# Transposes of the down product ahead of the Hadamard transposes, its products between them and the Hadamard products, in one feed forward of a twelve-block decoder

## The chip, the cores and the metric

The kernel runs on one core of one Trainium2 chip. A core has five engines that each work off a queue of their own in order: TensorE (PE in the rows; PEld is its weight load), VectorE (DVE), ScalarE (ACT), GpSimd (POOL) and SyncE (SP), which here only starts DMAs. The metric is the device time of one launch in microseconds, the median of several runs. One further execution was taken with the hardware profiler; all rows come from it.

## The reference

A decoder of four layers with an attention, a cross attention and a feed forward each, `x = layernorm(x + block(x))` twelve times, on `x` of shape (4, 512, 512) in float32. The change touches one block, the feed forward of the second layer, which works on quantised activations and ternary weights and has a Walsh-Hadamard transform of length 2048 in front of its last product:

```python
def act_quant(x, bits=8):
    qb = 128.0
    scale = qb / jnp.clip(jnp.max(jnp.abs(x), axis=-1, keepdims=True), EPS)
    return jnp.clip(jnp.round(x * scale), -qb, qb - 1) / scale

def bitlinear(x, w):
    return jnp.einsum('bsh,oh->bso', act_quant(x), weight_quant(w))

def h_bitlinear(x, w):
    return jnp.einsum('bsh,oh->bso', act_quant(fwht(x)), weight_quant(w))

gate = bitlinear(x, w_gate)          # 512 -> 2048
up = bitlinear(x, w_up)              # 512 -> 2048
return h_bitlinear(jax.nn.silu(gate) * up, w_down)   # 2048 -> 512
```

## The kernel before

The 2048 rows of `x` stay on the chip as 16 tiles of 128 rows. Each block is a stage between two barriers: every engine waits at its start until all engines and DMAs are done with the stage before. The stage of this change is `l1_ffn`. No DMA is on its path; the weights are there.

Each tile `i` runs through a pipeline of rounds `t`. The table `LAG` says how many rounds after its start a tile is at a step, and `order(names)` walks, in each round, through the named steps in the order in which they are named. Each engine has a string of names of its own, so this string is the order of that engine's queue. The steps of one tile are:

- quant: VectorE quantises the tile of `x`, ScalarE writes it as bf16 (XB, L1775).
- turn: TensorE transposes it (4 transposes, L210 by way of `k.tr`), ScalarE copies it (XT, L1744).
- up: TensorE makes gate and up in four column blocks each, `g` and `u` in turn, 4 products of 128x512 a block (L205 by way of `k.mm`); ScalarE applies silu to `g` (L1751), VectorE multiplies with `u` into IM (L1805), which frees the bank of `u`.
- hadamard: TensorE transposes IM (the it transposes, 16 of 128x128 f32), ScalarE copies them (L1756); TensorE multiplies with the 128x128 Hadamard matrix (the ha products, 16, shown as 32 rows), ScalarE copies these (L1760). The four remaining levels over the 16 blocks are butterflies (L1694): two on VectorE, four instructions, and two on GpSimd, four instructions.
- stats, scale, clip: VectorE reduces the maximum (L1818) and works out the scale (to L1826), ScalarE multiplies (L1765), VectorE clips (L1831), ScalarE writes bf16 (YB, L1770).
- down: TensorE transposes YB (the yt transposes, 16), ScalarE copies them in two halves (L1780), TensorE makes the 16 products of `y`, VectorE adds the residual into z (L1836) and goes on with the norm (L248, L250, L266; the reciprocal root between is GpSimd's, L256 and L259).

In round `t` TensorE works on hadamard of tile t-3, down of t-5, up of t-2 and turn of t-1.

All products and transposes land in the eight PSUM banks, which `Banks.take` hands out in turn; a take waits until the reader of that bank's last content is done:

```python
i = self.n % len(self.aps)
for engine, *what in self.by[i]:
    self.k.pe.wait_ge(engine, *what)
self.by[i], self.at[key] = by, i
```

A round takes 20 banks: 4 for it, 4 for ha, 2 for yt, 1 for `y`, 8 for `g` and `u`, 1 for turn. The bank of `y` is released by z.

Of the kernel before, what the change touches and what calls it, by code (L numbers as in the profile page):

```python
# [122 lines left out]
def quad(ap):  # L123
    return ap.rearrange("p (k n) -> p k n", k=4)
# [566 lines left out]
def l0_xattn(k):  # L691
# [17 lines left out]
    S1, S2, OB = k.banks(0, 2, 2), k.banks(4, 2), k.banks(6, 2)  # L709
    LAG = 20  # L710
    kv = kst[:, :, 0:96].rearrange("p h (r d) -> p h r d", d=16)
    qv = qst.rearrange("p h (r d) -> p h r d", d=16)

    def order():
# [5 lines left out]
        yield "qt", 0, 1  # L720
        for n in range(16 * NT + LAG + 11):
            i, j = divmod(n, 16)
# [12 lines left out]
            if 0 <= i < NT and j == 0:  # L735
                yield "maxrows", i, 0
            i, j = divmod(n - LAG, 16)
            if 0 <= i < NT:
# [915 lines left out]
def l1_ffn(k):  # L1654
# [20 lines left out]
    sc = k.bsc  # L1675
    HN = float(1.0 / np.sqrt(2048))

    LAG = dict(quant=0, turn=1, up=2, up2=2, hadamard=3, stats=4, scale=4, clip=4, down=5)

    def order(names):  # L1680

        for t in range(NT + 5):
            for what in names.split():
                if 0 <= t - LAG[what] < NT:
                    yield what, t - LAG[what]
# [8 lines left out]
        return f(o[:, :, 0 if op == ALU.add else 1, :], v[:, :, 0, :], v[:, :, 1, :], op)  # L1694

    def tensor():
        for what, i in order("hadamard down up turn"):
            if what == "turn":
                bb = eighths(R.take("xt", i, by=((act, "xt", i),)))
                pe.wait_ge(act, "xb", i)  # L1700
                for kk in range(4):
                    t = k.tr(bb[:, kk, :], XB[i % 2][:, kk * P:kk * P + P])
                t.then_inc(*pe.done("xt", i))
            elif what == "up":
                pe.wait_ge(act, "xt", i)
                for c in range(4):
                    for name, w, by in (("g", k.WG, act), ("u", k.WU, dve)):
                        r = R.take(name, i, c, by=((by, name, i, c),))
                        for kk in range(4):
                            t = k.mm(r, XT[i % 2][:, kk, :], w[:, kk, 512 * c:512 * c + 512], kk == 0, kk == 3)  # L1710
                        t.then_inc(*pe.done(name, i, c))
            elif what == "hadamard":
                pe.wait_ge(dve, "u", i, 3)
                for c in range(4):
                    bb = quad(R.take("it", i, c, by=((act, "it", i, c),)))
                    for j in range(4):
                        t = k.tr(bb[:, j, :], IM[i % 2][:, (4 * c + j) * P:(4 * c + j + 1) * P])
                    t.then_inc(*pe.done("it", i, c))
                for c in range(4):
                    r = R.take("ha", i, c, by=((act, "ha", i, c),))  # L1720
                    pe.wait_ge(act, "it", i, c)
                    for j in range(4):
                        t = k.mm(r[:, j * P:j * P + P], IT[:, 4 * c + j, :], k.HM, True, True)
                    t.then_inc(*pe.done("ha", i, c))
            elif what == "down":
                pe.wait_ge(act, "yb", i)
                for c in range(2):
                    bb = eighths(R.take("yt", i, c, by=((act, "yt", i, c),)))
                    for j in range(8):
                        t = k.tr(bb[:, j, :], YB[i % 2][:, (8 * c + j) * P:(8 * c + j + 1) * P])  # L1730
                    t.then_inc(*pe.done("yt", i, c))
                r = R.take("y", i, by=((dve, "z", i),))
                for j in range(16):
                    pe.wait_ge(act, "yt", i, j // 8)
                    t = k.mm(r, YT[i % 2][:, j, :], k.WD[:, j, :], j == 0, j == 15)
                t.then_inc(*pe.done("y", i))

    def scalar():
        for what, i in order("hadamard scale down up clip up2 turn quant"):
            m = sm[:, i, :]  # L1740
            if what == "turn":
                act.wait_ge(pe, "xt", i)
                act.wait_ge(pe, "u", i - 2, 3) if i >= 2 else None
                nc.scalar.activation(XT[i % 2], eighths(R.of("xt", i))[:, 0:4], ACT.Copy).then_inc(*act.done("xt", i))  # L1744
            elif what in ("up", "up2"):
                for c in (0, 1) if what == "up" else (2, 3):
                    n = 4 * i + c - 3
                    act.wait_ge(pe, "g", i, c)
                    act.wait_ge(dve, "fg", i)
                    act.wait_ge(dve, "u", n // 4, n % 4) if n >= 0 else None  # L1750
                    nc.scalar.activation(SG[n % 3], R.of("g", i, c), ACT.Silu, scale=sm[:, i, 2:3]).then_inc(*act.done("g", i, c))  # L1751
            elif what == "hadamard":
                for c in range(4):
                    act.wait_ge(pe, "it", i, c)
                    act.wait_ge(pe, "ha", i - 1, 3) if i else None
                    nc.scalar.activation(IT[:, 4 * c:4 * c + 4, :], quad(R.of("it", i, c)), ACT.Copy).then_inc(*act.done("it", i, c))  # L1756
                for c in range(4):
                    act.wait_ge(pe, "ha", i, c)
                    act.wait_ge(act, "yb", i - 2)
                    nc.scalar.activation(HA[i % 2][:, 512 * c:512 * c + 512], R.of("ha", i, c), ACT.Copy).then_inc(  # L1760
                        *act.done("ha", i, c))
            elif what == "scale":
                act.wait_ge(dve, "hscale", i)
                act.wait_ge(pool, "magic")
                nc.scalar.activation(HA[i % 2], HA[i % 2], ACT.Identity, bias=MG[:, 0:1], scale=m[:, 5:6]).then_inc(  # L1765
                    *act.done("rounded", i))
            elif what == "clip":
                act.wait_ge(dve, "clip", i)
                act.wait_ge(pe, "yt", i - 2, 1) if i >= 2 else None
                nc.scalar.activation(YB[i % 2], HA[i % 2], ACT.Identity, bias=MG[:, 1:2]).then_inc(*act.done("yb", i))  # L1770
            elif what == "quant":
                act.wait_ge(dve, "xq", i)
                act.wait_ge(pe, "xt", i - 2)
                act.wait_ge(pool, "magic")
                nc.scalar.activation(XB[i % 2], XQ[i % 2], ACT.Identity, bias=MG[:, 1:2]).then_inc(*act.done("xb", i))  # L1775
            elif what == "down":
                for c in range(2):
                    act.wait_ge(pe, "yt", i, c)
                    act.wait_ge(pe, "y", i - 2)
                    nc.scalar.activation(YT[i % 2][:, 8 * c:8 * c + 8, :], eighths(R.of("yt", i, c)), ACT.Copy).then_inc(  # L1780
                        *act.done("yt", i, c))
# [1488 lines left out]
```

## Time and profile before

| what | us |
|---|---|
| median of 3 runs | 5221.11 (5209.8 to 5226.85) |
| the profiled execution | 5222.23 |
| its span, first to last instruction | 5221.0 |
| TensorE, VectorE, ScalarE, GpSimd busy | 4487.0, 3036.8, 1674.0, 1651.4 |
| mean granted clock of TensorE | 0.927 of full |

The span is 1.2 us shorter than the execution's time. The busy times are sums over eleven stages with different limits. In the rows below, a line such as `2223.31 4.75 DVE L1694 TENSOR_TENSOR ... x4 [0.98 <-ACT arena L1760]` reads: VectorE started at 2223.31 us with four instructions of line 1694 that took 4.75 us together, and had been idle for 0.98 us before, until ScalarE's instruction of line 1760 released it. Ends of TensorE's instructions are modelled, so neighbouring rows can overlap a little.

### The profile page before, as it was taken

How to read it: one execution, taken by the hardware profiler on the slowest of the kernel's cores; microseconds unless marked ns; L12 is line 12 of the kernel's file. 1: busy time of each engine (PE TensorE's matmuls, PEld its weight loads, DVE VectorE, ACT ScalarE, POOL GpSimd, SP SyncE). 2: the span in 40 equal slices, each digit the busy share in tenths (PEclk: the TensorE clock that was granted, in tenths of full speed). 3: DMA queues.
4: the chain of work that ended last, by engine and by line, in shares of the span. 5: the costliest groups of instructions: out<-in, count | busy, mean ns of one | idle time of the engine just before them, and what ended most of it. 6: DMA issues, size and time to landing. Idle time of an engine off the chain costs nothing. (4 is left out here: it accounts for less than half of the span.)

```text
span 5221.0 us, 65766 instructions
## 1 busy us (share of the span) xinstructions
PE 4487.0 (86%) x23000; PEld 2381.0 (46%) x23000; DVE 3036.8 (58%) x5498; ACT 1674.0 (32%) x3306; POOL 1651.4 (32%) x1828
## 2 busy tenths in 40 slices
PE   6996888899998667887999888749999997997688
PEld 5773222244445443554333333325555554443466
DVE  5875777668777987884455565643333333565432
ACT  1112666622112325663222222201111111454332
POOL 1324222000114653552011113455555554112411
PEclk9997999999997678999999999969999998998699
DMA  4330000110000002000011110029999987001000
GB/s 144 92 93 10 2 2 2 44 45 1 0 1 1 0 10 112 1 1 29 29 30 56 30 49 21 22 75 222 238 236 233 218 194 178 10 1 45 2 15 19
DMA packets 154390, 327.67 MB, mean 63 GB/s; under 512 B 25841, under 2 KB 39665, under 8 KB 152498
## 3 DMA queue, kind: packets, MB, share of 16 engines
q1 hardware_dynamic: 107090, 222.90, 13.2%
q0 software_dynamic: 46976, 100.56, 9.9%
q8 instruction: 189, 3.10, 0.3%
q14 instruction: 135, 1.11, 0.1%
HBM read 377.91 MB, written 79.30 MB: 88 GB/s over the span
## 5 line engine op out<-in xcount | busy, mean ns | idle before, releaser
L205 PE MATMUL ps<-arena 128*128 128x512 f32 (+17 forms) x18744 | 3935.3, 451 | 450.3 <-ACT arena L1294 52.3
L205 PEld LDWEIGHTS ps<-arena 128*128 128x128 f32 (+6 forms) x18744 | 1855.3, 164 | 2331.4 <-issue 1210.6
L210 PE MATMUL ps<-arena 128*128 128x128 f32 (+2 forms) x3232 | 423.8, 271 | 245.5 <-DVE arena L266 51.3
L210 PEld LDWEIGHTS ps<-arena 128*128 128x128 f32 (+2 forms) x3232 | 346.5, 140 | 421.0 <-issue 195.1
L2871 POOL DMA_INDIRECT moe_y<-arena x191 | 304.7, 1595 | 303.2 <-DVE arena L2840 235.3
L256 POOL TENSOR_SCALAR arena<-arena 128x1 f32<-128x1 f32 x160 | 54.5, 340 | 982.5 <-DVE arena L250 980.6
L867 DVE TENSOR_REDUCE arena<-ps 128x2 f32<-128x1024 f32 x256 | 303.8, 1218 | 86.3 <-PE ps L205 85.6
L2400 ACT ACTIVATE arena<-ps 128x1024 f32<-128x1024 f32 (+3 forms) x256 | 166.2, 701 | 577.2 <-PE ps L205 569.2
L2426 DVE TENSOR_REDUCE arena<-ps 128x2 f32<-128x256 f32 (+3 forms) x256 | 199.0, 819 | 257.5 <-PE ps L205 257.5
L2823 DVE SCALAR_TENSOR_TENSOR arena<-ps,arena 128x128 f32<-128x128 f32 x382 | 103.6, 313 | 409.3 <-ACT arena L2810 343.9
L841 ACT ACTIVATE arena<-ps 128x512 f32<-128x512 f32 x512 | 277.7, 597 | 129.3 <-PE ps L205 126.7
L2468 POOL TENSOR_SCALAR_AFFINE_SELECT arena<-arena 128x512 f32<-128x512 f32 x128 | 81.7, 639 | 699.9 <-ACT arena L2400 699.8
L2810 ACT ACTIVATE arena<-ps 128x192 f32<-128x192 f32 x191 | 63.1, 330 | 687.4 <-PE ps L205 673.6
L205 PE MATMUL ps<-r,r 128*128 128x512 f32 x1024 | 248.5, 405 | 26.0 <-DVE r L3119 24.6
L2840 DVE COPY arena<-ps 128x512 f32<-128x512 f32 x191 | 123.1, 686 | 221.6 <-PE ps L205 221.6
L205 PEld LDWEIGHTS ps<-r,r 128*128 128x128 f32 x1024 | 198.2, 194 | 75.1 <-DVE r L3119 26.4
L2864 POOL DMA_INDIRECT arena<-moe_x,arena x191 | 189.5, 992 | 117.5 <-PE ps L210 71.1
L353 DVE MAX8 arena<-arena 128x8 f32<-128x512 f32 x304 | 211.3, 695 | 10.4
L1694 POOL TENSOR_TENSOR arena<-arena 128x1024 f32<-128x1024 f32 x64 | 164.5, 2590 | 161.7 <-DVE arena L1694 160.4
L351 DVE MATCH_REPLACE8 arena<-arena 128x512 f32<-128x512 f32 x304 | 205.3, 675 | 0.0
L2601 ACT ACTIVATE arena<-ps,arena 128x128 f32<-128x128 f32 (+3 forms) x256 | 131.6, 525 | 127.4 <-DVE arena L2629 126.7
L2626 DVE TENSOR_REDUCE arena<-ps 128x2 f32<-128x256 f32 (+3 forms) x128 | 104.9, 820 | 103.3 <-PE ps L205 103.3
(310 smaller groups left out, 3924.2 us busy)
## 6 DMA issues: line engine op xcount, KB each, us to landing
arena<-in_L_ffn_gu SPq DMA_DIRECT2D x191, 768.0 KB
arena<-in_L_ffn_dn SPq DMA_DIRECT2D x191, 256.0 KB
arena<-in_L_ffn_dn SPq DMA_DIRECT2D x191, 128.0 KB
arena<-in_L_ffn_w SPq DMA_DIRECT2D x64, 256.0 KB
moe_y<-arena SPq DMA_DIRECT2D x34, 256.0 KB
arena<-in_L_ffn_w_gate SPq DMA_DIRECT2D x32, 256.0 KB
arena<-in_L_ffn_w_up SPq DMA_DIRECT2D x32, 256.0 KB
arena<-in_L_ffn_w_down SPq DMA_DIRECT2D x32, 256.0 KB
```

What stands on the lines that cost most here:

```text
L205: return self.nc.tensor.matmul(out, lhsT, rhs, start=start, stop=stop, skip_group_check=True)
L210: return self.nc.tensor.transpose(out, in_, ident[0:n, 0:n])
L351: nc.vector.match_replace(k.tw, k.tm8, k.tw if j else s, -3.0e38).then_inc(*(dve.done() if j else dve.done("tfree", n)))
L353: nc.vector.max(k.tm8, k.tw).then_inc(*dve.done())
L841: nc.scalar.activation(PT[v][:, t4].rearrange("p h n -> p (h n)"), S2.of("s2", i, j), ACT.Exp).then_inc(*act.done("p", i, j))
L867: nc.vector.tensor_reduce(MX[:, i % 2, 2 * j:2 * j + 2], S1.of("s1", i, j), AX.X, ALU.max, negate=True).then_inc(*dve.done("mx", i, j))
L1694: return f(o[:, :, 0 if op == ALU.add else 1, :], v[:, :, 0, :], v[:, :, 1, :], op)
L2400: nc.scalar.activation(PT[n % 4][:, 2 * j:2 * j + 2, 0:512 - q0], S.of("s2", n, j)[:, :, 0:512 - q0], ACT.Exp, scale=SC).then_inc(*act.don ...
L2426: nc.vector.tensor_reduce(MX[:, i % 2, 2 * j:2 * j + 2, m], S.of("s1", n, j)[:, :, 0:keys], AX.X, ALU.max, negate=True).then_inc(*dve.done ...
L2601: nc.scalar.activation(JK[g % 2][:, 0:keys], S.of("s", n, g // 2)[:, g % 2, 0:keys], ACT.Exp, bias=SM[:, i % 2, 0, h:h + 1], scale=SC, acc ...
L2864: nc.gpsimd.indirect_dma_start(XG[n % NX], None, XD, bass.IndirectOffsetOnAxis(ap=TT[:, n:n + 1].bitcast(U32), axis=0)).then_inc(rows_in[n ...
L2871: nc.gpsimd.indirect_dma_start(YD[n % 2], bass.IndirectOffsetOnAxis(ap=TT[:, n:n + 1].bitcast(U32), axis=0), YG[n % 4], None, compute_op=A ...
```

## The change

The step hadamard is split in two on TensorE, `it` and `ha`, with the same lag as before, and the step down is split in two on TensorE, `back` (the yt transposes) and `down` (the products of `y`), with the same lag as before. In TensorE's queue a round was: it, ha, yt, y, up, turn; it is now: yt, it, y, ha, up, turn. In ScalarE's queue the copies of yt stood behind hadamard and scale; they stand in front of hadamard now. VectorE's and GpSimd's orders stay.

```diff
-    LAG = dict(quant=0, turn=1, up=2, up2=2, hadamard=3, stats=4, scale=4, clip=4, down=5)
+    LAG = dict(quant=0, turn=1, up=2, up2=2, hadamard=3, it=3, ha=3, stats=4, scale=4, clip=4, back=5, down=5)
...
     def tensor():
-        for what, i in order("hadamard down up turn"):
+        for what, i in order("back it down ha up turn"):
...
-            elif what == "hadamard":
+            elif what == "it":
                 pe.wait_ge(dve, "u", i, 3)
                 for c in range(4):
                     bb = quad(R.take("it", i, c, by=((act, "it", i, c),)))
                     for j in range(4):
                         t = k.tr(bb[:, j, :], IM[i % 2][:, (4 * c + j) * P:(4 * c + j + 1) * P])
                     t.then_inc(*pe.done("it", i, c))
+            elif what == "ha":
                 for c in range(4):
                     r = R.take("ha", i, c, by=((act, "ha", i, c),))
                     pe.wait_ge(act, "it", i, c)
...
-            elif what == "down":
+            elif what == "back":
                 pe.wait_ge(act, "yb", i)
                 for c in range(2):
                     bb = eighths(R.take("yt", i, c, by=((act, "yt", i, c),)))
                     for j in range(8):
                         t = k.tr(bb[:, j, :], YB[i % 2][:, (8 * c + j) * P:(8 * c + j + 1) * P])
                     t.then_inc(*pe.done("yt", i, c))
+            elif what == "down":
                 r = R.take("y", i, by=((dve, "z", i),))
                 for j in range(16):
                     pe.wait_ge(act, "yt", i, j // 8)
...
     def scalar():
-        for what, i in order("hadamard scale down up clip up2 turn quant"):
+        for what, i in order("back hadamard scale up clip up2 turn quant"):
...
-            elif what == "down":
+            elif what == "back":
                 for c in range(2):
                     act.wait_ge(pe, "yt", i, c)
```

TensorE's queue over one round of the middle of the stage, the rows of before with -, those of the change with +. `128x128` rows of L210 are transposes, `128x128` rows of L205 the ha products, `128x512` rows the products of y and of up:

```order
 L205 MATMUL ps<-arena 128x128 x16
 L205 MATMUL ps<-arena 128x512 x32
-L210 MATMUL ps<-arena 128x128 x20
+L210 MATMUL ps<-arena 128x128 x36
+L205 MATMUL ps<-arena 128x512 x16
 L205 MATMUL ps<-arena 128x128 x16
-L210 MATMUL ps<-arena 128x128 x16
-L205 MATMUL ps<-arena 128x512 x48
```

The 16 yt transposes moved from behind the ha products to the turn and it transposes (20 become 36), and the 16 products of y from behind ha to in front of it.

The same queue with its waits, from the ha products on, in the same round. A row's wait is that of its first instruction:

```order
-L210 MATMUL ps<-arena 128x128 x16
-L205 MATMUL ps<-arena 128x512 [waits l1ffn_act_done]
-L205 MATMUL ps<-arena 128x512 x7
-L205 MATMUL ps<-arena 128x512 [waits l1ffn_act_done]
-L205 MATMUL ps<-arena 128x512 x35
+L205 MATMUL ps<-arena 128x512 x12
 L205 MATMUL ps<-arena 128x512 [waits l1ffn_dve_done]
 L205 MATMUL ps<-arena 128x512 x3
```

The wait for VectorE is that for the bank of y. It stood in front of the last four products of up (the block u3); it now stands behind the first twelve of them, in front of u1.

ScalarE's queue over one round, first before:

```order
L1756 ACTIVATE arena<-ps 128x512 x4
L1760 ACTIVATE arena<-ps 128x512 x4
L1765 ACTIVATE arena<-arena 128x2048
L1780 ACTIVATE arena<-ps 128x1024 x2
L1751 ACTIVATE arena<-ps,arena 128x512 x2
L1770 ACTIVATE arena<-arena 128x2048
```

and of the change, where every line number is two higher:

```order
L1782 ACTIVATE arena<-ps 128x1024 x2
L1758 ACTIVATE arena<-ps 128x512 x4
L1762 ACTIVATE arena<-ps 128x512 x4
L1767 ACTIVATE arena<-arena 128x2048
L1753 ACTIVATE arena<-ps,arena 128x512 x2
L1772 ACTIVATE arena<-arena 128x2048
```

The two copies of yt (L1780, now L1782) moved from behind the scale to in front of the it copies.

## Rows read from the trace of the kernel before

**Rows 1.** The page's first part: busy time of each engine over the span.

```profile
PE 4487.0 (86%) x23000; PEld 2381.0 (46%) x23000; DVE 3036.8 (58%) x5498; ACT 1674.0 (32%) x3306; POOL 1651.4 (32%) x1828
```

**Rows 2.** Windows: busy us (instructions) of PE, PEld, DVE, ACT, POOL; granted clock; DMA.

```profile
2135.00:2381.00 246.00, 206.06 (x1388) 133.75 (x1388) 208.78 (x299) 166.85 (x215) 134.22 (x71) 1.00 0.00 1
```

**Rows 3.** Timeline of one round, 2216 to 2238 us.

```profile
2216.10 0.39 PE L210 MATMUL ps<-arena 128*128 128x128 bf16 x4
...
2217.11 1.97 PE L210 MATMUL ps<-arena 128*128 128x128 f32 x16 [0.62 <-DVE arena L1805]
...
2218.91 3.74 PE L205 MATMUL ps<-arena 128*128 128x128 f32 x32
...
2222.48 1.06 PE L210 MATMUL ps<-arena 128*128 128x128 bf16 x16
...
2223.18 2.08 ACT L1765 ACTIVATE arena<-arena 128x2048 f32<-128x2048 f32 x1
2223.31 4.75 DVE L1694 TENSOR_TENSOR arena<-arena 128x1024 f32<-128x1024 f32 x4 [0.98 <-ACT arena L1760]
2225.16 1.93 ACT L1780 ACTIVATE arena<-ps 128x1024 bf16<-128x1024 bf16 x2
...
2226.23 10.53 PE L205 MATMUL ps<-arena 128*128 128x512 bf16 x48 [2.69 <-ACT arena L1780]
2227.98 1.22 DVE L1831 TENSOR_SCALAR arena<-arena 128x2048 f32<-128x2048 f32 x1
...
2229.89 0.75 DVE L1836 SCALAR_TENSOR_TENSOR arena<-ps,arena 128x512 f32<-128x512 f32 x1 [0.69 <-PE ps L205]
...
2231.51 2.50 DVE L266 TENSOR_SCALAR arena<-arena 128x512 f32<-128x512 f32 x1
...
2233.07 1.99 ACT L1770 ACTIVATE arena<-arena 128x2048 bf16<-128x2048 f32 x1
2233.93 1.40 DVE L1805 SCALAR_TENSOR_TENSOR arena<-ps,arena 128x512 f32<-128x512 f32 x2
...
2236.80 0.75 DVE L1805 SCALAR_TENSOR_TENSOR arena<-ps,arena 128x512 f32<-128x512 f32 x1 [0.31 <-PE ps L205]
...
2237.61 1.97 PE L210 MATMUL ps<-arena 128*128 128x128 f32 x16 [0.62 <-DVE arena L1805]
```

**Rows 4.** First quant step of the stage; timeline of the it transposes, two rounds.

```profile
2060.88 0.69 DVE L1787 TENSOR_REDUCE arena<-arena 128x1 f32<-128x512 f32 x1 [2.20 <-ACT arena L1556]
...
2135.10 1.97 PE L210 MATMUL ps<-arena 128*128 128x128 f32 x16 [0.62 <-DVE arena L1805]
...
2381.12 1.97 PE L210 MATMUL ps<-arena 128*128 128x128 f32 x16 [0.85 <-DVE arena L1805]
```

**Rows 5.** Waits, 2060 to 2424 us: total, times, longest.

```profile
PE ps L205 <- ACT arena L1780: 50.6, 16, 12.3
```

**Rows 6.** Timeline and windows (as Rows 2) of two stretches early in the stage.

```profile
2110.24 3.67 PE L210 MATMUL ps<-arena 128*128 128x128 f32 x16 [6.94 <-DVE arena L1805]
...
2122.03 12.22 PE L205 MATMUL ps<-arena 128*128 128x512 bf16 x48 [2.69 <-ACT arena L1780]
...
2122.80:2126.10 3.30, 3.30 (x9) 1.15 (x8) 2.21 (x2) 0.09 (x1) 2.15 (x1) 0.51 0.02 5
...
2110.20:2113.60 3.40, 3.36 (x16) 3.36 (x17) 3.26 (x7) 1.84 (x4) 3.32 (x3) 0.50 0.00 0
```

**Rows 7.** Timeline of the stage's drain.

```profile
2408.68 5.63 PE L205 MATMUL ps<-arena 128*128 128x512 bf16 x16 [12.31 <-ACT arena L1780]
...
2415.88 3.63 PE L205 MATMUL ps<-arena 128*128 128x512 bf16 x16 [0.67 <-ACT arena L1780]
2415.97 0.52 DVE L266 TENSOR_SCALAR arena<-arena 128x512 f32<-128x512 f32 x1
...
2422.39 0.55 DVE L266 TENSOR_SCALAR arena<-arena 128x512 f32<-128x512 f32 x1 [0.71 <-POOL arena L259]
```

**Rows 8.** Timeline of GpSimd's first and second butterfly in the round before Rows 3.

```profile
2207.64 3.27 POOL L1694 TENSOR_TENSOR arena<-arena 128x1024 f32<-128x1024 f32 x1 [8.85 <-DVE arena L1694]
...
2210.88 2.34 POOL L1694 TENSOR_TENSOR arena<-arena 128x1024 f32<-128x1024 f32 x1
```

## Prediction

> **What bounds the kernel now.** The page comes first: TensorE (PE in the rows) is busy for 86% of the span [rows 1], but the change touches only the stage of the second feed forward, which begins at 2060.9 us and ends at 2422.9 us, between two barriers [rows 4, 7]; nothing else can move except by a shift. The windows view over the middle of that stage is next [rows 2]: between 2135 and 2381 us TensorE is busy for 206 of 246 us, VectorE (DVE) for 209, ScalarE (ACT) for 167, GpSimd (POOL) for 134, and TensorE's granted clock is 1.00, the 2.4 GHz level. No engine is full, so waits set the pace, and a busy share doesn't tell which.
>
> The timeline shows one round of the pipeline, word for word the same in the rounds before and after it [rows 3]. The it transposes of round t start at 2217.11 and those of the next at 2237.61: 20.50 us. Over the stage the same step stands at 2135.10 and at 2381.12, twelve rounds later [rows 4]: (2381.12 - 2135.10) / 12 = 20.50. Inside the round the reader is to see two idle times on TensorE: 2.69 us in front of the 48 products (16 of down, 32 of up), which wait for ScalarE's copy of the yt transposes (L1780), and 0.62 us in front of it, which waits for VectorE's last up product (L1805). The waits view sums the first to 50.6 us in 16 waits, of which one of 12.3 is in the drain [rows 5]. So the ring that sets the pace is: it, ha, ScalarE's four ha copies, its scale (2.08 us), its first yt copy, 48 products, u, it. VectorE stands beside it with small idle times only: 0.98 us in front of the Hadamard steps and 0.69 us in front of z [rows 3].
>
> **The change.** It adds and removes no instruction in the stage: the same 16 yt transposes, 16 y products, 16 it transposes, 16 ha products and two ScalarE copies a round stand in another order on two engines, and no DMA is moved. It does two things.
>
> First, yt goes ahead of it, and the yt copies ahead of the it copies. The clipped tile that yt needs (L1770) is ready 2.5 us before it begins (2233.07 + 1.99 against 2237.61) [rows 3]. The transposes fit into the 0.62 us wait nearly for nothing (16 take 1.06 us), ScalarE does the two copies (1.93 us) while TensorE does the 16 it transposes, and the 2.69 us wait goes. The scale no longer stands before any yt copy.
>
> Second, the 16 y products stand between it and ha. One product of 512 columns takes 10.53 / 48 = 0.219 us [rows 3], so ha starts 3.51 us later than it otherwise would. Behind ha stand ScalarE's ha copies and behind them VectorE's Hadamard steps, clip, z and up products, in that order on one queue. What is late next is thus VectorE.
>
> I count the new round from the start of it, T. The it transposes take 1.80 us (2217.11 to 2218.91), y 3.51, so ha starts at T + 5.31. The Hadamard steps start 4.40 us after ha does (2218.91 to 2223.31): T + 9.71, against T + 6.20 now. Clip starts 4.67 us after them (2223.31 to 2227.98) and takes 1.22; z now waits 0.69 us for TensorE's y, but y will have been done since T + 8.9, so z runs directly, from about T + 15.56, for 0.75 us, to T + 16.31 [rows 3].
>
> Here the banks come in. The eight PSUM banks are handed out in turn, and each round takes 20, so a bank's next user is the eighth take behind. Before, y was the eighth take in front of u3, the last of the up products. Now y is taken ahead of the four ha banks, and the eighth take behind it is u1, the fourth of eight up groups. The order of instructions shows it: the wait for VectorE stands behind 35 and eight more products before, behind 12 after ha now. That bank is free when z has read it. TensorE reaches it early: ha takes 3.57 us (2218.91 to 2222.48), to T + 8.88, g0, u0 and g1 take 12 x 0.219 = 2.63, to T + 11.51. It then waits until T + 16.37: a new wait of 4.9 us, where 2.69 + 0.62 stood. The rest is 20 products (4.39 us), 4 turn and 16 yt transposes (about 1.2 us by the 1.06 for 16), and it starts again at T + 22.0. VectorE's u3 would be done at T + 21.6, just hidden. **The round becomes 22.0 us, 1.5 longer.**
>
> Twelve rounds give 12 x 1.5 = +18.0. The round before them (it at 2110.24, 24.86 us to the next) contains half-clock stretches and an empty VectorE; I count it as unchanged, give or take 1.5. In the last round with ha the copies of tile 15 come 3.5 us later with no stall behind to swallow it: +3.5. In the drain y of tile 14 now runs early instead of at 2408.68, so the last yt starts sooner; but TensorE will be at half clock for the last y, whose 16 products then take 5.63 us as y(14) does now, not 3.63 [rows 7]: I take -1.0, with 0 and -3 as ends. Sum at full clock: 18.0 + 3.5 - 1.0 = **+20.5 us**.
>
> **The clock.** After an idle time of 6.94 us the it transposes at 2110.24 take 3.67 us for 16 instead of 1.97, and the granted clock there is 0.50, the 1.2 GHz level [rows 6]. After one of 2.69 us at 2122 the clock is 0.51 and the 48 products take 12.22 us, 1.69 more than 10.53. The twelve later waits of 2.69 us do not bring it down [rows 2]. The new wait of 4.9 us lies between: I expect the fall in most rounds. It then slows the 20 products behind the wait, and these are on the path. At 1.69 us in each of twelve it is +20; part of the slow stretch can lie inside the wait itself and a few rounds may escape, so I take 1.2 us: +14. Ends: 0 and +20. The Trainium skill ("TensorE: Matmul & The Clock Gate", section "HAM oscillation — how this bites in real kernels") says that a loop with an idle time in each turn can start every burst cold; by that rule the sum would take the full +20. The trace agrees at 2110 and 2408 and not in the twelve short waits.
>
> Total: 20.5 + 14 = +34.5. The profiled execution took 5222.2 us, 1.2 more than its span and 1.1 above the median of 5221.1 that I set the forecast against: 5221.1 + 34.5 = **5256 us**.
>
> **Rivals.** (a) The wait of 4.9 us leaves the clock up, as the 2.69 us waits do: +20.5, 5242. It needs the busy stretches on both sides to be enough. With the drain's and first round's ends it is +16 to +22.
> (b) VectorE is held by GpSimd. The normalisation L266 takes 2.50 us in the round but 0.52 when GpSimd is idle [rows 3, 7]: it starts at 2231.51, inside GpSimd's second butterfly instruction. In the preceding round the first ran from 2207.64 for 3.27 us and the second from 2210.88 for 2.34 [rows 3, 8]; L266, at 2211.01 there by the same period, ended when the second had. With z not waiting, L266 comes 0.69 us earlier relative to clip, at 2210.3 on that scale, inside the first, and ends with it, after about 0.9 us. My sum takes this. If it still meets the second, u3 ends about 2.3 us later than VectorE could otherwise have it, at T + 23.4, and the round is 23.5: 12 x 3.0 + 2.5 = +38.5, 5260. A lower clock adds nothing to it, since TensorE's products would then end at T + 22.5 at the latest, under VectorE's 23.4. The Trainium skill ("GPSIMD Engine Reference", section "Specifications") has GpSimd share its SBUF interfaces with VectorE, in contention for VectorE instructions in a two-port mode. By that rule either instruction of GpSimd can hold L266, and the trace agrees (2.50 against 0.52 us).
> (c) On the other side: the kernel gets faster. TensorE works for only 20.50 - 2.69 - 0.62 = 17.2 us a round; if nothing took the place of the two waits, 3.3 us a round or 12 x 3.3 = 40 us would go, 5181. It decides on whether the 3.51 us of y in front of ha are hidden on VectorE's ring. That ring, without any bank, is 9.71 to the Hadamard steps, 4.67 + 1.22 to the end of clip, 0.75 z, 0.87 to L266 (2229.89 + 0.75 to 2231.51), 0.9 L266, 4 x 0.70 up products (two take 1.40): 20.9 us. It is above 20.50 already, so it would have to lose another 0.4 us before anything is gained. Little speaks for it.
> (d) Little change: the drain and the first round give back 5 us or more and the clock stays up, or ha's delay is partly covered: 5221 to 5235.
>
> **How the numbers follow.** The main case (late z holds u1, clock falls in most rounds) has 0.58; (a) 0.20, of which a third ends within 0.3% (15.7 us, about what a measurement of this kernel can tell from no change); (b) 0.10; (c) 0.04; (d) 0.08, nearly all within. So faster 0.04, same 0.13, slower 0.83. The main case alone reaches from 5245 to 5265: the upper end is the full +20 for the clock, +1.5 for the first round and 0 for the drain. The range starts at (a) less its 5 us, 5236, and ends at that upper end plus half of what a measurement can shift, 5272; (c), most of (d) and the far ends, about 0.18, are outside.
>
> **What the changed profile would show.** In the middle of the stage: the it transposes 22 to 24 us apart; no wait of TensorE for the yt copies; a wait of 4.5 to 5 us of TensorE for VectorE's z (L1838, the former L1836) inside the up products, after twelve of them; yt directly behind turn; the Hadamard steps 9.7 us behind it; L266 near 0.9 us, not 2.5. For the clock: a granted clock below 1.00 in the windows view of the same stretch, and products 0.43 us apart behind the wait. I'm wrong in mechanism if the wait behind g1 is missing or short, or if z is not the last thing before u1; wrong in size if the clock stays 1.00 (then 5242), or if L266 stays at 2.5 us.

## The result, and the profile after

The changed kernel takes 5262.01 us in the median (5258.87 to 5263.23, 4 runs) against 5222.5 us (5209.8 to 5226.85, 4 runs) of the kernel before on the same chip. The ratio is 1.0077, 95% interval 1.0065 to 1.0089: 39.5 us slower. The forecast was 34.5 us slower, in a range of 5236 to 5272.

The page of the changed kernel gives the span, and the busy time of each engine over it, to be read against [rows 1].

```profile
span 5262.0 us, 65701 instructions
...
PE 4511.0 (86%) x22922; PEld 2391.6 (45%) x23000; DVE 3015.0 (57%) x5498; ACT 1673.4 (32%) x3306; POOL 1654.2 (31%) x1828
```

The amount of work is that of before: the weight loads are 23000 in both, and the 22922 products against 23000 are records that this trace lacks. The busy sum of TensorE grew by 24 us, though no product was added: the same products took longer. Where, the windows view of the changed kernel shows, first in the stretch of [rows 2] and then in three short ones of a single round.

```profile
2135.00:2381.00 246.00, 198.03 (x1193) 121.74 (x1212) 164.63 (x267) 143.81 (x188) 117.37 (x63) 0.86 0.00 1
...
2197.90:2199.80 1.90, 0.00 (x0) 0.00 (x0) 1.90 (x3) 0.58 (x1) 1.67 (x1) 0.50 0.00 0
2199.90:2204.20 4.30, 4.30 (x11) 1.55 (x12) 3.07 (x5) 1.99 (x2) 4.22 (x3) 0.50 0.02 4
2204.60:2206.40 1.80, 1.80 (x10) 0.85 (x9) 0.75 (x1) 0.56 (x1) 1.80 (x2) 1.00 0.00 0
```

In 246 us TensorE now gets through 1193 instructions where it got through 1388, and VectorE through 267 instead of 299: there are fewer rounds in the same time. The granted clock is 0.86 where it was 1.00. The three short rows say how that mean comes about. TensorE waits from 2195.2 to 2199.90 in that round, and the clock is already at 0.50, the 1.2 GHz level, in the last 2 us of the wait; it stays there behind the wait, while 11 products take 4.30 us, and is at 1.00, the 2.4 GHz level, right after them. From about 2197.9 to 2204.6 that is 6.7 us at half the clock in a round of 23.9, which gives the mean of 0.86.

The timeline of one round of the changed kernel answers to [rows 3].

```profile
2206.51 3.04 PE L210 MATMUL ps<-arena 128*128 128x128 bf16 x36
2206.71 0.75 DVE L1807 SCALAR_TENSOR_TENSOR arena<-ps,arena 128x512 f32<-128x512 f32 x1 [0.98 <-PE ps L205]
...
2208.04 1.93 ACT L1782 ACTIVATE arena<-ps 128x1024 bf16<-128x1024 bf16 x2
...
2209.60 9.56 PE L205 MATMUL ps<-arena 128*128 128x512 bf16 x58
...
2217.24 4.76 DVE L1694 TENSOR_TENSOR arena<-arena 128x1024 f32<-128x1024 f32 x4 [4.49 <-ACT arena L1762]
...
2221.91 1.22 DVE L1833 TENSOR_SCALAR arena<-arena 128x2048 f32<-128x2048 f32 x1
2222.07 10.52 POOL L1694 TENSOR_TENSOR arena<-arena 128x1024 f32<-128x1024 f32 x4 [12.36 <-DVE arena L1694]
...
2223.04 0.75 DVE L1838 SCALAR_TENSOR_TENSOR arena<-ps,arena 128x512 f32<-128x512 f32 x1
...
2223.84 6.74 PE L205 MATMUL ps<-arena 128*128 128x512 bf16 x20 [4.69 <-DVE arena L1838]
2224.65 0.98 DVE L266 TENSOR_SCALAR arena<-arena 128x512 f32<-128x512 f32 x1
...
2230.43 3.04 PE L210 MATMUL ps<-arena 128*128 128x128 bf16 x36
```

The x36 row is 4 turn, 16 yt and 16 it transposes in one piece, and it comes again after 2230.43 - 2206.51 = 23.92 us. The two idle times of before are gone. In their place TensorE waits 4.69 us for VectorE's z, inside the up products: z ends at 2223.04 + 0.75 = 2223.79, and the products go on at 2223.84. VectorE now waits 4.49 us in front of the Hadamard steps, where it waited 0.98.

Those waits, summed over the stage by the waits view of the changed kernel, take the place of [rows 5].

```profile
PE ps L205 <- DVE arena L1838: 60.9, 13, 4.7
...
DVE arena L1694 <- ACT arena L1762: 66.9, 15, 5.3
```

The starts of the Hadamard steps serve as marks, since they stand in every kernel below. Here are the fourth and the last one of the changed kernel, and the rows of its drain that answer to [rows 7].

```profile
2145.22 1.23 DVE L1694 TENSOR_TENSOR arena<-arena 128x1024 f32<-128x1024 f32 x1 [4.49 <-ACT arena L1762]
...
2432.26 4.75 DVE L1694 TENSOR_TENSOR arena<-arena 128x1024 f32<-128x1024 f32 x4 [5.27 <-ACT arena L1762]
...
2442.80 3.74 PE L205 MATMUL ps<-arena 128*128 128x512 bf16 x15 [0.67 <-ACT arena L1782]
...
2458.28 4.73 PE L205 MATMUL ps<-arena 128*128 128x512 bf16 x16 [0.26 <-ACT arena L1782]
...
2465.89 0.55 DVE L266 TENSOR_SCALAR arena<-arena 128x512 f32<-128x512 f32 x1 [0.72 <-POOL arena L259]
```

Twelve rounds lie between: 2432.26 - 2145.22 = 287.0 us, 23.92 each, against 246.0 before (2141.31 to 2387.32). The stage as a whole went from 362.1 to 405.5 us:

| part of the stage | before | after | difference | forecast |
|---|---|---|---|---|
| three rounds, first to fourth Hadamard start (the first is at 2082.6 in both) | 58.8 | 62.6 | +3.9 | +3.5 (put at the last round) |
| twelve rounds | 246.0 | 287.0 | +41.0 | +32 (18 and 14 for the clock) |
| drain, from the last Hadamard start | 35.6 | 34.2 | -1.4 | -1.0 |
| stage | 362.1 | 405.5 | +43.4 | +34.5 |

The parts leave out the 21.7 us in front of the first Hadamard start, which are alike. The span grew by 41.0 us, 2.4 less than the stage. What gave these 2.4 us back outside it was not found; in the traces below, the same code in front of the stage ends anywhere between 2055.7 and 2061.1 us, so one execution differs from another by as much.

### The profile page after: what moved, and what is told of

It is laid out like the page before. It is cut to its first block and busy times, and to the rows that moved or that the text cites. A ratio compares the mean times of both kernels' runs of the same rounds, so it can differ in the third digit from the quotient of the medians.

```text
span 5262.0 us, 65701 instructions
## 1 busy us (share of the span) xinstructions
PE 4511.0 (86%) x22922; PEld 2391.6 (45%) x23000; DVE 3015.0 (57%) x5498; ACT 1673.4 (32%) x3306; POOL 1654.2 (31%) x1828
## 5 line engine op out<-in xcount | busy, mean ns | idle before, releaser
L205 PE MATMUL ps<-arena 128*128 128x512 f32 (+19 forms) x18666 | 3955.2, 453 | 461.0 <-DVE arena L1838 60.9
L205 PEld LDWEIGHTS ps<-arena 128*128 128x128 f32 (+6 forms) x18744 | 1864.6, 165 | 2358.2 <-issue 1245.7
L210 PE MATMUL ps<-arena 128*128 128x128 f32 (+2 forms) x3232 | 421.0, 272 | 251.9 <-DVE arena L266 51.9
L210 PEld LDWEIGHTS ps<-arena 128*128 128x128 f32 (+2 forms) x3232 | 346.7, 141 | 424.6 <-issue 198.0
L205 PE MATMUL ps<-r,r 128*128 128x512 f32 x1024 | 248.4, 405 | 26.0 <-DVE r L3121 24.6
L205 PEld LDWEIGHTS ps<-r,r 128*128 128x128 f32 x1024 | 198.2, 194 | 75.0 <-DVE r L3121 26.4
```

The source lines that it names most:

```text
L205: return self.nc.tensor.matmul(out, lhsT, rhs, start=start, stop=stop, skip_group_check=True)
L210: return self.nc.tensor.transpose(out, in_, ident[0:n, 0:n])
```

## The experiments

The kernels of one group ran on one chip, beside runs of the kernel before on that chip. Every ratio is to those. The expectations are in microseconds of a kernel before at 5217 to 5222; where the chip of a group was slower, the ratio is what answers them.

**First group: the two parts of the change apart, the bank, the clock, the order on VectorE.** The kernel before took 5217.0 us here (median of 18).

*yt ahead only.* The 16 y products go back behind ha; all else stays as changed.

```diff
-        for what, i in order("back it down ha up turn"):
+        for what, i in order("back it ha down up turn"):
```

> One part of the change alone: the yt transposes and their copies stay ahead of the it transposes, but the products of y go back behind ha. Theory (y in front of ha costs, through late Hadamard steps and the bank of y): the 4.7 us wait for z goes, the bank of y again stands before u3, the granted clock is 1.00 in the middle of the stage. ScalarE's two yt copies now stand before the it copies, so the Hadamard steps start 6.6 us after it instead of 6.2; the 2.69 us wait is gone, and the round ends on VectorE and GpSimd at about 20.1 us. 5222.5 - 12 x 0.4 - 3 = 5214 (5206 to 5224). Rival (the new place of the yt copies is what costs): it stays above 5240.

Measured: 5192.71 us (5192.17 to 5196.76), ratio 0.9956 (0.9940 to 0.9973). It is faster than before, and by more than expected. The timeline of this kernel gives its round, and the windows view the middle of the stage.

```profile
2221.05 1.97 PE L210 MATMUL ps<-arena 128*128 128x128 f32 x16 [0.83 <-DVE arena L1807]
...
2223.26 14.20 PE L205 MATMUL ps<-arena 128*128 128x128 f32 x80 [0.25 <-ACT arena L1758]
...
2228.79 4.75 DVE L1694 TENSOR_TENSOR arena<-arena 128x1024 f32<-128x1024 f32 x4
...
2233.62 10.71 POOL L1694 TENSOR_TENSOR arena<-arena 128x1024 f32<-128x1024 f32 x4 [7.13 <-DVE arena L1694]
...
2239.86 1.97 PE L210 MATMUL ps<-arena 128*128 128x128 f32 x16 [0.83 <-DVE arena L1807]
```

```profile
2140.00:2360.00 220.00, 203.22 (x1365) 131.95 (x1364) 202.81 (x288) 162.11 (x211) 136.10 (x72) 1.00 0.00 1
```

The round is 18.81 us, the clock 1.00, and ha, y and the up products run through in one piece of 80. So all of the loss, and more than it, belongs to one part of the change, the place of y between it and ha: 5262 against 5193, by the two ratios, of two chips, 1.0077 - 0.9956 = 0.0121 or 63 us.

*An own bank for y.* As changed, but y has one PSUM bank to itself and the others share seven, so that no up product comes to stand behind z.

```diff
-    R = k.banks(0, 8)
+    R, YR = k.banks(0, 7), k.banks(7, 1)
...
-                r = R.take("y", i, by=((dve, "z", i),))
+                r = YR.take("y", i, by=((dve, "z", i),))
```

> The changed kernel with a PSUM bank of its own for y, the other takes going round over seven banks. Theory (the bank of y holds u1 until z): TensorE's wait of 4.7 us for z is gone; what is left is VectorE's own ring of 20.9 to 21.3 us, because the Hadamard steps still start 9.4 us after it. 5222.5 + 12 x 0.7 + 3 = 5234 (5228 to 5244; the upper end if the clock still falls in half of the rounds). Rival (VectorE's lateness alone makes the round, the bank only shows it): the round stays above 21.5 us at full clock and the time within 5 us of 5262.

Measured: 5228.64 us (5225.58 to 5234.3), ratio 1.0023 (1.0013 to 1.0033). The timeline and then the windows view of this kernel:

```profile
2215.11 1.29 PE L210 MATMUL ps<-arena 128*128 128x128 bf16 x20 [2.86 <-DVE arena L1807]
...
2217.09 1.97 PE L210 MATMUL ps<-arena 128*128 128x128 f32 x16 [0.68 <-DVE arena L1807]
...
2235.85 1.29 PE L210 MATMUL ps<-arena 128*128 128x128 bf16 x20 [2.86 <-DVE arena L1807]
...
2237.82 3.42 PE L210 MATMUL ps<-arena 128*128 128x128 f32 x16 [0.68 <-DVE arena L1807]
```

```profile
2140.00:2360.00 220.00, 187.95 (x1185) 125.68 (x1184) 184.18 (x257) 141.20 (x185) 114.06 (x60) 0.94 0.00 1
```

The wait for z is gone, and with it 0.54% of the time (1.0077 to 1.0023). What is left is a wait for VectorE's up products, 2.86 and 0.68 us. At the full clock a round takes 20.74 us (2215.11 to 2235.85), close to VectorE's ring of 20.9 that the prediction worked out. Over the twelve rounds that begin at the fourth Hadamard start the mean is 21.6, because the clock still falls in ten of them: two take 20.72 and 20.73 us, the others 21.08 to 22.41. The 16 it transposes at 2237.82 take 3.42 us where those at 2217.09 take 1.97.

*The wait filled.* As changed, but the four products of g1 are issued five times over, 16 more of them a round, in front of the wait. The repeats make g1 anew, so only time is added.

```diff
-                        for kk in range(4):
+                        for kk in list(range(4)) * (5 if (name, c) == ("g", 1) and i >= 3 else 1):
```

> The changed kernel, but TensorE makes the four products of the gate block g1 five times over (16 products more a tile, from tile 3 on; the same result is written again), 3.5 us of work put into the 4.7 us wait for z. It tests the clock alone. Theory (the idle time brings the clock down and the half-clock products behind it cost 2.35 us a round): the granted clock is 1.00 in the middle of the stage, the round falls from 23.9 to 21.6 us, and the kernel with more work is faster: 5262 - 12 x 2.3 = 5234 (5230 to 5242). Rival (the clock comes down for another reason, or the slow products are hidden): the round stays at 23.9 or grows, 5262 or more.

Measured: 5233.07 us (5230.36 to 5239.46), ratio 1.0039 (1.0027 to 1.0052). The timeline of this kernel over a round, and the windows view:

```profile
2205.44 4.75 DVE L1694 TENSOR_TENSOR arena<-arena 128x1024 f32<-128x1024 f32 x4 [2.46 <-ACT arena L1762]
...
2212.05 4.49 PE L205 MATMUL ps<-arena 128*128 128x512 bf16 x20 [1.23 <-DVE arena L1838]
...
2227.10 4.75 DVE L1694 TENSOR_TENSOR arena<-arena 128x1024 f32<-128x1024 f32 x4 [2.45 <-ACT arena L1762]
```

```profile
2140.00:2360.00 220.00, 207.69 (x1338) 128.51 (x1336) 179.45 (x256) 141.76 (x183) 114.27 (x60) 1.00 0.00 1
```

More work, less time: with 16 needless products a round the kernel is 0.38% faster than the changed one. The wait is 1.23 us instead of 4.69, the clock 1.00, the 20 products behind it take 4.49 us instead of 6.74, and the round is 2227.10 - 2205.44 = 21.66 us. This splits the 3.42 us that a round of the changed kernel lost: 21.66 - 20.50 = 1.16 by the new order, 23.92 - 21.66 = 2.26 by the clock.

*z ahead of the Hadamard steps.* As changed, but VectorE does z, and the normalisation's first steps with it, in front of the Hadamard steps.

```diff
-        for what, i in order("quant stats hadamard clip down up"):
+        for what, i in order("quant stats down hadamard clip up"):
```

> The changed kernel with z and its norm moved on VectorE's queue from behind clip to in front of the Hadamard steps. y is done 5.3 us after it, the Hadamard steps start at 9.4, so z fits into VectorE's idle time and u1 never waits. Theory: the wait for z goes and the clock stays at 1.00; but z, statistics and L266 now stand between stats and the Hadamard steps, and stats waits for GpSimd, so the ring of VectorE and GpSimd (butterflies 10.4, stats 3.1, z and norm 2.4, Hadamard steps 4.75) gives about 21.3 to 21.7 us: 5236 (5228 to 5244). Rival (GpSimd's ring is not closed): 20.0 us a round and 5216.

Measured: 5227.31 us (5225.02 to 5232.4), ratio 1.0021 (1.0009 to 1.0033); a little better than expected, and within the interval of own bank. Its waits view shows where TensorE stands now, and its windows view the clock.

```profile
PE ps L210 <- ACT arena L1772: 46.5, 16, 8.8
```

```profile
2140.00:2360.00 220.00, 190.17 (x1193) 126.92 (x1192) 189.01 (x260) 141.19 (x186) 118.01 (x63) 0.92 0.00 1
```

The bank is free early, and TensorE waits for ScalarE's cast of the clipped tile instead, which is late because clip is. The clock was expected to stay at 1.00 and did not: it is 0.92. Where a round loses nothing by it, the Hadamard starts are some 20.65 us apart, under the 21.3 to 21.7 expected; the mean of twelve is 21.3. Two ways of taking the wait for z away thus end at the same place: the Hadamard steps come late, and something behind them is waited for.

**Second group: is it the transposes or the scale, and what does a later y cost?** The kernel before took 5232.31 us here (median of 13).

*Scale behind yt.* The kernel before, with ScalarE's scale moved behind its yt copies and nothing else changed: the 2.69 us wait should go without any change on TensorE.

```diff
-        for what, i in order("hadamard scale down up clip up2 turn quant"):
+        for what, i in order("hadamard down scale up clip up2 turn quant"):
```

> The kernel before with one name moved: on ScalarE's queue the two yt copies stand in front of the scale, still behind ha's copies; TensorE's order is untouched (it, ha, yt, y, up, turn). Theory: what paid in moving yt ahead was that its copy no longer waits for the 2.08 us scale, not that the transposes come first. y then starts 7.2 us after it instead of 9.1, z does not wait, L266 meets GpSimd's first butterfly instruction, and the round ends, as in the kernel with yt ahead alone, on GpSimd's butterflies (10.7), stats (3.2) and the Hadamard steps (4.75): 18.8 us. 5217 - 12 x 1.7 = 5197, 5192 to 5203. Rival (the transposes ahead of it are what frees the round): 20.0 us or more a round and above 5210.

Measured: 5203.14 us (5199.4 to 5207.09), ratio 0.9944 (0.9927 to 0.9960), or 29 us where 20 were expected. The wait for the yt copies is 0.94 us, down from 2.69. The timeline of this kernel:

```profile
2199.80 10.73 POOL L1694 TENSOR_TENSOR arena<-arena 128x1024 f32<-128x1024 f32 x4 [7.13 <-DVE arena L1694]
...
2210.73 2.27 DVE L1818 TENSOR_REDUCE arena<-arena 128x1 f32<-128x2048 f32 x1
...
2213.81 4.74 DVE L1694 TENSOR_TENSOR arena<-arena 128x1024 f32<-128x1024 f32 x4
...
2218.63 10.73 POOL L1694 TENSOR_TENSOR arena<-arena 128x1024 f32<-128x1024 f32 x4 [7.14 <-DVE arena L1694]
```

One edit on one engine's list gives the same round, 18.83 us, as yt ahead did. The reader sees what bounds it: GpSimd's four butterflies (10.73), VectorE's reduction of their result (2.27, with five small steps behind it some 3.1), VectorE's four butterflies (4.74), and GpSimd again with the next tile. TensorE is no longer in the ring: what it still waits costs nothing.

*y twice, own bank.* As in own bank, with the 16 y products issued twice. 3.5 us more stand between it and ha. The second pass starts the sum anew, since `j == 0` is the product's start flag; so only time is added, and y does not come out doubled as the two expectations say.

```diff
-                for j in range(16):
+                for j in list(range(16)) * 2:
```

> The changed kernel with a bank of its own for y, and the 16 products of y made twice (y comes out doubled). It doubles the term of 3.5 us in front of ha with the bank out of the way. Theory (all of y's time in front of ha lies on VectorE's ring): the round grows by 3.5 us from 20.7 to 24.2, 5228.6 + 12 x 3.5 + 4 = 5275 (5265 to 5285). Rival (VectorE's idle time takes up part, or the bank was all): under 5255.

Measured: 5299.9 us (5298.3 to 5303.31), ratio 1.0130 (1.0113 to 1.0147): 1.07% or 56 us above own bank. Its stage has no round at the full clock, so like is compared with like: the second and third intervals between Hadamard starts are 24.19 and 24.10 us, against 20.73 and 20.67 in own bank, 3.4 longer and nearly all of the 3.51 us of y, with a clock of 0.93 against 0.92 in the third. Later rounds take 25.0 and 26.2 in turn, 25.6 in the mean of twelve against 21.6. Its timeline and windows show the wait of VectorE and the clock.

```profile
2223.39 4.75 DVE L1694 TENSOR_TENSOR arena<-arena 128x1024 f32<-128x1024 f32 x4 [7.29 <-ACT arena L1762]
```

```profile
2121.90:2146.00 24.10, 22.03 (x131) 14.22 (x132) 18.35 (x25) 13.54 (x19) 11.25 (x6) 0.93 0.00 1
2140.00:2360.00 220.00, 192.67 (x1114) 125.96 (x1129) 157.81 (x223) 118.43 (x154) 95.73 (x50) 0.90 0.00 1
```

*y twice, behind ha.* As in yt ahead only, with the same second pass over the y products.

> The kernel with yt ahead alone (y behind ha), and the 16 products of y made twice (y comes out doubled): the same extra work, but behind ha. Theory: it no longer delays the Hadamard steps; TensorE idles about 1.4 us of the round of 18.8, so it fills that first and then TensorE is the bound at about 20.9 to 21.2 us. 5192.7 + 12 x 2.2 + 4 = 5223 (5214 to 5236), half or less of what the same products cost in front of ha. Rival (the place does not matter): +46, 5239 or more.

Measured: 5241.36 us (5237.99 to 5248.15), ratio 1.0018 (1.0008 to 1.0027): 0.62% or 32 us above yt ahead only. The bare 5241 us would fall to the rival (5239 or more), but the kernel before is 15 us slower on this chip than the one that the expectation counts from; the ratio lies inside the theory's range (5214 to 5236 over 5217 is 0.9994 to 1.0036) and below the rival's 1.0042. Its rounds take 21.48 us at a clock of 1.00, 2.66 more than 18.82. So there was a slack of 0.85 us for TensorE in that place and none between it and ha.

**Third group: a repeat of the two fast ones, and a further step.** The kernel before took 5229.19 us here (median of 15).

*yt ahead, again* and *scale behind yt, again*, side by side on one chip, to tell them apart.

> The kernel with yt ahead alone once more, beside the next two on one chip: 18.8 us a round, a ratio to before of 0.9945 to 0.996.

> The kernel before with the scale behind the yt copies once more. Both rounds are 18.8 us in the trace, so if the transposes' place adds nothing the two ratios agree within 0.1%; if yt ahead saves something of its own in the first and last rounds, this one is 3 to 8 us slower.

Measured: 5206.82 us (5198.25 to 5210.26), ratio 0.9957 (0.9944 to 0.9971), and 5203.32 us (5194.28 to 5210.43), ratio 0.9949 (0.9936 to 0.9963). The intervals overlap: no difference that can be told. The transposes' new place adds nothing to what the scale's place gives.

*One butterfly more on VectorE.* From yt ahead only: the sums of the second level go from GpSimd, which bounds the ring, to VectorE, which has room.

```diff
+                dve.wait_ge(dve, "b1", i)
+                butterfly(nc.vector.tensor_tensor, i, 2, ALU.add).then_inc(*dve.done("b2v", i))
...
-                butterfly(nc.gpsimd.tensor_tensor, i, 2, ALU.add).then_inc(*pool.done("b2", i))
...
+                pool.wait_ge(dve, "b2v", i)
```

> The kernel with yt ahead alone, and one of GpSimd's four butterfly instructions (level 2, the sums) on VectorE. Theory A (GpSimd's butterflies, stats and the Hadamard steps close the round of 18.8, and nothing else is near): GpSimd is done 2.4 us sooner, VectorE has 1.2 us more: 17.6 to 18.0 us a round, 10 to 14 us faster. Theory B (VectorE's own ring from it over ha, Hadamard steps, clip, z and the up products stands just under it, at 6.5 + 4.7 + 1.2 + 0.75 + 0.9 + 1.0 + 2.7 = 17.7 us, and grows by 1.2 to 18.9): no gain, within 3 us of the kernel with yt ahead. I hold B for likelier, at 0.6.

Measured: 5236.82 us (5230.23 to 5243.1), ratio 1.0016 (1.0007 to 1.0025): 30 us slower than yt ahead, where neither theory expected a loss. The timeline of this kernel shows what is late, and the windows view, over two rounds, what the clock does.

```profile
2225.48 6.01 DVE L1694 TENSOR_TENSOR arena<-arena 128x1024 f32<-128x1024 f32 x5 [1.60 <-ACT arena L1762]
2230.31 3.39 POOL L1694 TENSOR_TENSOR arena<-arena 128x1024 f32<-128x1024 f32 x1 [11.23 <-DVE arena L1694]
2231.41 3.38 DVE L1835 TENSOR_SCALAR arena<-arena 128x2048 f32<-128x2048 f32 x1
```

```profile
2182.93:2204.15 21.22, 17.61 (x117) 11.14 (x116) 19.32 (x27) 13.78 (x19) 9.86 (x5) 1.00 0.00 1
...
2225.48:2247.83 22.35, 19.00 (x117) 12.76 (x116) 19.30 (x27) 13.99 (x19) 9.86 (x5) 0.92 0.00 1
```

GpSimd may start once its inputs are there, which is now ahead of VectorE's fifth butterfly. Its first instruction takes 3.39 us, and clip (L1835 here), which starts 1.1 us into it, takes 3.38 us where it takes 1.22 in every kernel above: it starts there 0.16 us ahead of GpSimd, here inside. The clipped tile comes 2.2 us late in addition to the 1.2 us of the fifth butterfly, and the rounds are 21.2 to 22.4 us. At the full clock a round takes 21.22 us, 2.4 more than with yt ahead; the longer ones lose up to 1.1 us more by the clock, at 0.92. That clip's hold is the larger part of the 2.4 is read from the timeline; no run has the fifth butterfly without it.

## Why the prediction was right, and where its sizes were off

**The round.** The steps stood where they were put. In the frame of the prediction (T at about 2207.8, 1.80 us ahead of y at 2209.60) the Hadamard steps came at T + 9.4 (predicted 9.71), z at T + 15.2 (15.56), the waiting products at T + 16.0 (16.37), and the wait was 4.69 us (4.9). That z's bank is the cause is shown by own bank, where the wait is gone. That the place of y is what makes the Hadamard steps late is shown by y twice in its two places, +3.4 us and +2.66 us a round, and by yt ahead only, where the loss turns into a gain. The full-clock round was 21.66 us in the kernel with the wait filled, not 22.0: 1.16 us a round and 13.9 in twelve, where the term said 18.0. The working had each mark 0.3 us late, and this is what it was off by. One time in it is a slip: y "done since T + 8.9" should read T + 5.3 by its own numbers; z didn't wait for y in either case.

**The clock.** This term was mis-sized: 14 us predicted, with +20 as its upper end, and 12 x 2.26 = 27.1 us measured, by the changed kernel against the wait filled. The step that was off is the price of a round, 1.69 us at the upper end and 1.2 taken, because "part of the slow stretch can lie inside the wait itself and a few rounds may escape". No round escaped: the twelve take 23.83 to 24.08 us each. Part of the slow stretch does lie inside the wait, some 2 us of it, but the stretch is 6.7 us long, so 4.7 us of it are left for the products behind, where 11 products took 4.30 us and, at the full clock, ten took 1.80. Two weight loads of these products in the timeline of the changed kernel stand 0.42 us apart, as the prediction had it (0.43):

```profile
2224.68 0.15 PEld L205 LDWEIGHTS ps<-arena 128*128 128x128 bf16 x1 [0.28 <-issue]
2225.10 0.15 PEld L205 LDWEIGHTS ps<-arena 128*128 128x128 bf16 x1 [0.28 <-issue]
```

The upper end was too low as well, since it was taken from the one row where 48 products lost 1.69 us, in a slow stretch of some 3.4 us [rows 6]; here 20 products took 6.74 us, 2.25 more than the 4.49 with the wait filled. The rule of the Trainium skill ("TensorE: Matmul & The Clock Gate", section "HAM oscillation — how this bites in real kernels"), that a loop with an idle time in each turn can start every burst cold, agrees with the changed kernel in every round, where the rows give 2.26 us as its price. Its example is a loop with waits as long as the 4.69 us here, which the prediction did not say; the 2.69 us waits of the kernel before, which left the clock at 1.00, are shorter, and so are those of own bank, none above 2.9 us, which brought it down in ten rounds of twelve. For such waits the measurement decides.

**The ends.** The extra of the last round, +3.5, is there at +3.9, but at the first rounds: they too have Hadamard steps later by y's length. The drain gave -1.4 (predicted -1.0); its last y took 4.73 us, not the 5.63 of the working. The two errors of size, -4.1 and +13.1, make the stage some 9 us longer than forecast; the rest of the span gave 2.4 us back, and the medians (+39.5) stand 1.5 us closer than the spans of the two profiled executions (+41.0). So the sum came out 5 us short. The mechanism is right; that 5262 lies so near to 5256 is in part luck, since the two errors have opposite signs and 3.9 us came back for no reason that the runs show.

**The rivals.** (a) The clock stays up: fallen, it was 0.86. The wait filled is that case made by hand, and it lies at 1.0039, or +20 us (14 to 27 by its interval); (a) said +20.5. Its trace has 13.9 us in the twelve rounds, where (a) has 18, and a stage of 375.4 us, 13.3 more than before, so part of that agreement is chance. (b) L266 held by GpSimd's second instruction: fallen, it started 2.6 us into the first and took 0.98 us (2224.65, against 2.50 in [rows 3]). (c) Faster: fallen, because the round without the bank is 20.7 us by own bank (worked out as 20.9), above 20.50. (d) Little change: fallen.

**What the prediction didn't see** is that the first part of the change, by itself, is worth 24 us. It named the 2.69 us wait as the thing that goes, but weighed both parts only together. In ratios the two parts are worth -0.0044 and +0.0121.

## What to carry to other kernels

Price each part of a combined change alone: here the half that pays (-24 us) was the one line that takes a long ScalarE step out from in front of a short one that TensorE waits for, and the other half cost 63 us. Work that fills an engine costs its full length when it is put in front of the step that feeds a chain through other engines, and here 0.85 us less than that when it stands behind it. Where buffers are handed out in turn, moving one product also moves which later product waits for its reader; look up who takes that buffer next. Of the versions run, the scale behind yt (0.9944 and 0.9949) or yt ahead alone (0.9956 and 0.9957) beat both kernels; their next bound is the ring of GpSimd and VectorE, 18.8 us.

## What was not expected of the hardware

An idle time of TensorE can cost more than itself: 4.69 us in each round brought the granted clock to 0.50, and 11 products then took 4.30 us; 16 needless products in front of the wait bought back 2.26 us a round. Between the two lies a case that stays open: the twelve waits of 2.69 us of before never lowered the clock, while the waits of 2.86 and 0.68 us of own bank did in ten rounds of twelve (clock 0.94 in the middle of the stage). The length of the longest wait does not decide it: in the kernel with one butterfly more on VectorE no wait in the middle of the stage is longer than 1.33 us, three of them (1.19, 1.33 and 0.83) stand within 6 us, and the clock fell to a mean of 0.92 in rounds such as the one shown above. Nor do the waits alone: the rows of own bank around 2217 and 2237 show the same waits, 2.86 and 0.68 us, around the same 20 transposes, and the 16 behind them take 1.97 us the first time and 3.42 the second. No run here separates the length of the waits from the work between them.

Elementwise instructions of VectorE and of GpSimd hold each other up. Clip takes 1.22 us when it starts ahead of GpSimd's first butterfly. When it starts inside, it takes 3.38: GpSimd's instruction is over at 2230.31 + 3.39 = 2233.70, and clip 1.09 us after that, at 2234.79, so nearly all of its work waited. The view of the butterfly's line in the kernel with one more of them on VectorE, over some two rounds, shows the other direction (after the colon the shortest, median and longest in ns):

```profile
L1694 DVE TENSOR_TENSOR arena<-arena x15: 1218/1224/1226, 2204.2 to 2252.6; 128x1024 f32<-128x1024 f32 x15
...
L1694 POOL TENSOR_TENSOR arena<-arena x9: 2536/3221/3389, 2209.0 to 2259.3; 128x1024 f32<-128x1024 f32 x9
```

VectorE's butterflies, with two inputs in SBUF, keep their 1.22 us, and GpSimd's first of each round takes 3.39 beside one of them, as it takes 3.27 beside clip in [rows 8], against 2.34 for its second there. The Trainium skill ("GPSIMD Engine Reference", section "Specifications") names both kinds of VectorE instruction, those in a two-port mode and those with two SBUF inputs, as in contention with GpSimd. The trace agrees for the butterflies, which have two SBUF inputs; in which mode clip and L266 run, no row says. It adds who pays: GpSimd beside VectorE's butterfly or behind clip's start, VectorE when clip or L266 starts inside GpSimd's instruction.
